# A feed-forward attention tail hosted by the first expert unit, and closer routing stages between two expert units

## What is computed

```python
x = x + 0.5 * ffn(layernorm(x))      # three tree-routed MLPs give q, k, v (16 leaves of width 64),
                                     # then softmax(q k^T / sqrt(128)) v with one head of 128
x = x + attention(layernorm(x))      # 16 heads, rotary positions, alibi, causal
x = x + 0.5 * ffn(layernorm(x))
x = x + 0.5 * moe(layernorm(x))      # softmax gate, top 2 of 8 experts, and a shared MLP; each MLP is
                                     # (silu(x w1) * (x w3)) w2, inner width 256
x = x + mamba(layernorm(x))          # selective scan, 16 states
x = x + 0.5 * moe(layernorm(x))
```

## Time and profile before

| | |
|---|---|
| median of 3 runs | 1473.67 us (1473.6 to 1476.0) |
| the profiled execution | 1469.0 us |
| span of the profiled execution | 1467.2 us |
| granted TensorE clock, mean | 0.945 |
| busy PE / DVE / ACT / POOL | 83% / 68% / 41% / 17% |
| second ffn unit's tail in front of the experts | twice, at 358 and at 1081 us |
| first expert unit of a layer | begins at 369.5, 653.9, 1093.0 and 1377.3 us |
| second expert unit of a layer | begins at 413.8, 697.5, 1137.1 and 1420.9 us |

### The profile page before, as it was taken

How to read it: one execution, slowest core, us unless ns; L and a number is a source line. 1 busy time by engine, 2 the same in 40 slices (tenths; PEclk the granted TensorE clock), 3 DMA queues, 4 the chain that set the end, 5 groups by cost and what they waited for, 6 DMA issues and landing times.

```text
span 1467.2 us, 16299 instructions
## 1 busy us (share of the span) xinstructions
PE 1214.4 (83%) x5655; PEld 743.9 (51%) x5704; DVE 1000.6 (68%) x1944; ACT 596.4 (41%) x995; POOL 242.3 (17%) x211
## 2 busy tenths in 40 slices
PE   5997888998997575669999977889989956747798
PEld 3675444676664122236667644446766622312465
DVE  6666665555685996977764775645557769889765
ACT  4542455344224345422234424543432254455222
POOL 3001000000200461631000010000001015536110
PEclk9999899999999797999999999999999978979999
DMA  6203110001010000010100122100010100000110
GB/s 207 58 25 98 51 55 2 1 1 44 15 58 0 1 0 0 1 58 1 65 23 1 49 54 74 32 2 0 1 58 1 58 1 0 0 0 1 58 62 11
DMA packets 27315, 45.06 MB, mean 31 GB/s; under 512 B 3649, under 2 KB 19297, under 8 KB 27041
## 3 DMA queue, kind: packets, MB, share of 16 engines
q1 hardware_dynamic: 27232, 44.02, 9.5%
HBM read 36.34 MB, written 8.19 MB: 30 GB/s over the span
## 4 chain that ended last, share of the span: by engine, by line
PE 62%; DVE 21%; issue 8%; ACT 5%; DMA 2%; POOL 2%; SPq 1%; POOLq 0%; DVEq 0%; another core or an unknown queue 0%; ACTq 0%
PE bank L1385 12%; PE bank L1387 11%; PE bank L1386 11%; PE bank L1546 8%; DVE n_h L1353 4%; PE bank L1394 3%; DVE a_mx L1291 3%; DVE bank L1345 3%; PE bank L1463 2%; PE bank L1609 2%; PE bank L1519 2%; PE bank L1705 1%; PE bank L1580 1%; POOL n_hc L751 1%; PE bank L1647 1%
## 5 line engine op out<-in xcount | busy, mean ns | idle before, releaser
L1141 DVE SCALAR_TENSOR_TENSOR f_hl<-bank,f_hh 128x512 fp32r<-128x512 f32 x192 | 131.5, 689 | 125.0 <-ACT f_hh L817 124.1
L817 ACT ACTIVATE f_hh<-bank 128x512 fp32r<-128x512 f32 x192 | 114.7, 597 | 197.0 <-PE bank L1463 151.2
L751 POOL TENSOR_TENSOR n_hc<-n_h,n_cs 128x512 f32<-128x512 f32 x128 | 160.4, 1270 | 141.2 <-DVE n_h L1353 93.1
L876 ACT ACTIVATE m_sl<-bank 128x512 f32<-128x512 f32 x144 | 85.8, 597 | 220.0 <-PE bank L1387 219.5
L1385 PE MATMUL bank<-xT_h,mw_h 128*128 128x512 f32 x288 | 160.6, 558 | 7.0 <-DVEq L495 4.3
L1705 PE MATMUL bank<-n_hc,ident 128*128 128x512 f32 x256 | 143.5, 679 | 11.6 <-POOL n_hc L751 10.8
L1353 DVE TENSOR_TENSOR_SCAN n_h<-n_da,bank 128x512 f32<-128x512 f32 x128 | 149.6, 1206 | 4.6 <-POOL n_hc L751 4.5
L1546 PE MATMUL bank<-m_h,mw 128*128 128x512 f32 x288 | 145.6, 594 | 0.0
L969 ACT ACTIVATE n_da<-n_dt,amat 128x512 f32<-128x512 f32 x128 | 91.7, 721 | 131.9 <-DVE n_h L1353 124.9
L1291 DVE TENSOR_REDUCE a_mx<-bank 128x1 f32<-128x384 f32 (+3 forms) x176 | 106.2, 638 | 50.4 <-PE bank L1649 48.0
L1203 DVE TENSOR_TENSOR m_t<-m_sl,bank 128x512 f32<-128x512 f32 x128 | 87.9, 686 | 73.4 <-PE bank L1387 72.8
(11 more groups left out here) (231 smaller groups left out, 2381.2 us busy)
## 6 DMA issues: line engine op xcount, KB each, us to landing
m_c<-comb_dram SPq DMA_DIRECT2D x28, 512.0 KB, 5.0
a_q<-stack_dram SPq DMA_DIRECT2D x8, 512.0 KB, 3.8
a_k<-stack_dram SPq DMA_DIRECT2D x16, 256.0 KB, 5.2
stage_fw<-in_fw_dram SPq DMA_DIRECT2D x6, 512.0 KB, 8.1
stack_dram<-R SPq DMA_DIRECT2D x16, 192.0 KB, 2.9
w_stage<-in_mw_dram SPq DMA_DIRECT2D x9, 256.0 KB, 2.7
stack_dram<-R SPq DMA_DIRECT2D x16, 128.0 KB, 2.6
m_c0b<-comb_dram SPq DMA_DIRECT2D x4, 512.0 KB, 3.4
```

Of the source, the lines that this page charges most:

```text
L751: n_hcs.by(nc.gpsimd.tensor_tensor(n_hc[:, m, :], n_h[:, m, :], n_cs[:, n // 2 % 2, :], ALU.mult))
L817: f_hi.by(act.activation(f_h[0][:, i % 4, :], bank[:, i % 3, :], ACT.Relu))
L1141: f_lo.by(V.scalar_tensor_tensor(f_h[1][:, i % 4, :], bank[:, i % 3, :], 0.0, f_h[0][:, i % 4, :].bitcast(F32), ALU.max, ALU.subtract))
```

## The change

It does two things. First, a second ffn unit that an expert unit follows ends without a barrier, and the expert unit hosts its tail in steps 0 to 7 by the plan above (units 5 to 6 and 17 to 18). The expert unit therefore hosts the stages of its own successor with a lag of 7. Second, where an expert unit hosts the stages of an expert unit (units 6, 10, 18 and 22 host for 7, 11, 19 and 23), the stages stand closer by new tables: ranks and combine are one stage (`choice`), the four exps are one stage of POOL. PSUM banks are dealt anew: product b uses 2 and 7, the w2 sums bank 3 (slot 0) or 6 (slot 1), the turned sums bank 4, the stages bank 5 where the host is an expert unit. Two DMA waits are replaced.

```diff
-POOL_STAGES = {0: "guess", 3: "rms", 8: "exp 0", 9: "exp 1", 10: "exp 2", 11: "exp 3"}
+POOL_STAGES = {0: "guess", 3: "rms"}
+PAIR_DVE_STAGES = {0: "stats", 1: "rows", 4: "low", 6: "first", 8: "fourth", 9: "choice", 10: "row"}
+PAIR_POOL_STAGES = {0: "guess", 6: "exps"}
+PAIR_ACT_STAGES = {4: "high"}
+PAIR_PE_STAGES = {3: "turn", 5: "first", 11: "weights"}
...
-            return UNITS[u] in (("ffn", 0), ("moe", 0), ("mha", 0))
+            return UNITS[u] in (("ffn", 0), ("moe", 0), ("mha", 0)) or tail_follows(u)
+
+        def tail_follows(u):
+
+            return UNITS[u] == ("ffn", 1) and u + 1 < NU and UNITS[u + 1][0] == "moe"
+
+        def moe_lag(u):
+            if UNITS[u][1] == 1:
+                return MOE_LAG
+            return FFN_LAG if tail_follows(u - 1) else 0
+
+        def stage_bank(u):
+
+            return 5 if u and UNITS[u - 1][0] == "moe" else 7
+
+        def y_bank(p):
+            return (3, 6)[p]
+
+        Y_ROWS = 4
...
-                        sp.wait_ge(unit_done, done_before(UNITS_OF_EXPERTS[k]))
+                        sp.wait_ge(m_s2.sem, m_s2.at(k, 8))
+                    if p == 1 and n == 3:
+
+                        sp.wait_ge(m_hs.sem, m_hs.at(k - 1, 14))
...
-                if stage in EXPS and kind == "moe" and UNITS[u - 1][0] == "moe":
-
-                    t = EXPS.index(stage)
+                if stage == "exps":
+
                     pool.wait_ge(e_sub.sem, e_sub.at(k, 0))
-                    e_exp.by(nc.gpsimd.tensor_tensor(gexp[:, t], euler[:, t], glog[:, t], ALU.pow))
+                    for t in range(NT):
+                        e_exp.by(nc.gpsimd.tensor_tensor(gexp[:, t], euler[:, t], glog[:, t], ALU.pow))
...
-                if p == 0:
+                if runs_on(u):
                     return
                 copy_pT(k, 1)
...
-                    hand_over(u, i - MOE_LAG * p)
+                    hand_over(u, i - moe_lag(u))
+                    if tail_follows(u - 1):
+                        kf = kth[u - 1]
+                        if i in (2, 4):
+                            copy_pT(kf, i // 2)
+                            probs(kf, i // 2 + 1)
+                        if i == 6:
+                            copy_pT(kf, 3)
                 act.wait_ge(m_s2.sem, m_s2.at(k, MSTEPS - 1))
-                m_y.by(act.activation(m_yT[:], bank[:, 6, :], ACT.Copy))
+                m_y.by(act.activation(m_yT[:], bank[:, y_bank(p), :], ACT.Copy))
...
+                    if tail_follows(u - 1):
+                        kf = kth[u - 1]
+                        if i == 0:
+                            rows_of_v(kf)
+                        if i in (1, 3):
+                            score_max(kf, 2 + i // 2)
+                        if i == 7:
+                            weighted(kf, batch_of(u - 1))
+                    hand_over(u, i - moe_lag(u))
...
-                if p == 1:
+                if p == 1 and not runs_on(u):
                     attend(k, [item for at in sorted(ATTEND_AT) for item in ATTEND_AT[at]])
...
-                        m_b.by(product(bank[:, 2 + i % 2, :], [mw[c][:, e, 2 + m, :] for c in range(2)], x))
+                        if i == 1:
+
+                            pe.wait_ge(e_row.sem, e_row.at(k, 0))
+                        m_b.by(product(bank[:, (2, 7)[i % 2], :], [mw[c][:, e, 2 + m, :] for c in range(2)], x))
...
-                        if i2 == 0 and p == 1:
-
-                            pe.wait_ge(m_y.sem, m_y.at(k - 1, 0))
-                        m_s2.by(mm(bank[:, 6, :], mw2[:, e, m, :], m_h[:, i2 % 3, :],
+                        if i2 == 0 and tail_follows(u - 1):
+
+                            pe.wait_ge(f_vok.sem, f_vok.at(kth[u - 1], 0))
+                        m_s2.by(mm(bank[:, y_bank(p), :], mw2[:, e, m, :], m_h[:, i2 % 3, :],
                                    start=i2 == 0, stop=i2 == MSTEPS - 1))
-                    if i == 1:
-
-                        pe.wait_ge(e_row.sem, e_row.at(k, 0))
-                    hand_over(u, i - MOE_LAG * p)
+                    if tail_follows(u - 1):
+                        attend(kth[u - 1], ATTEND_AT.get(i, ()))
+                    hand_over(u, i - moe_lag(u))
```

More of the change, by code:

```diff
@@ L121 @@
              5: [("weigh", 0), ("weigh", 1), ("weigh", 2), ("turn", 3)], 7: [("weigh", 3)]}
-EXPS = [f"exp {t}" for t in range(NT)]
 HEAD_PARTS = [f"{side} {c}" for side in "qk" for c in range(3)]
@@ L126, with stage_at @@
 HEAD_LAG = {0: -6, 1: 11}
-def stage_at(table, i, kind):
+def stage_at(table, i, kind, host):
     late = ("turn", "high", "low")
@@ L135, in stage_at @@
                 return ahead.get(i)
+    if kind == "moe" and host == "moe":
+        for own, pair in ((DVE_STAGES, PAIR_DVE_STAGES), (POOL_STAGES, PAIR_POOL_STAGES),
+                          (ACT_STAGES, PAIR_ACT_STAGES), (PE_STAGES, PAIR_PE_STAGES)):
+            if table is own:
+                return pair.get(i)
     if kind == "mamba":
@@ L789, in prologue @@
                     act.wait_ge(g_tr.sem, g_tr.at(u, 0))
-                    g_xh.by(act.activation(xT[0][:, p, :], bank[:, 7, :], ACT.Copy,
+                    g_xh.by(act.activation(xT[0][:, p, :], bank[:, stage_bank(u), :], ACT.Copy,
                                            scale=norm_w if kind == "mamba" else 1.0))
@@ L1099, in prologue @@
                         scores()
-                    if stage == "ranks":
+                    if stage in ("ranks", "choice"):
                         ranks(cmp[p])
-                    if stage == "combine":
+                    if stage in ("combine", "choice"):
                         combine()
@@ L1202, in moe @@
                     if e < EXPERTS:
-                        m_ts.by(V.tensor_tensor(m_t[:, m, :], m_sl[:, m, :], bank[:, 2 + m, :], ALU.mult))
+                        m_ts.by(V.tensor_tensor(m_t[:, m, :], m_sl[:, m, :], bank[:, (2, 7)[m], :], ALU.mult))
                         dve.wait_ge(m_ts.sem, m_ts.at(k, 2 * e + m))
@@ L1412, in prologue @@
                         pe.wait_ge(g_xl.sem, g_xl.at(u, 0))
-                        t_sc.by(product(bank[0:96, 7, :], [rw[0][:, 0:96], rw[1][:, 0:96]], xs(p)))
+                        t_sc.by(product(bank[0:96, stage_bank(u), :], [rw[0][:, 0:96], rw[1][:, 0:96]], xs(p)))
                     if stage == "second":
                         pe.wait_ge(t_bit.sem, t_bit.at(k, 0))
-                        t_cnt.by(mm(bank[:, 7, :], tree[:, 0, :], dbit[:], start=True, stop=True))
+                        t_cnt.by(mm(bank[:, stage_bank(u), :], tree[:, 0, :], dbit[:], start=True, stop=True))
                     if stage in ("third", "fourth"):
@@ L1558, in rows_of_y @@
                 pe.wait_ge(m_y.sem, m_y.at(k, 0))
-                m_ytr.by(back(7, m_yT))
+                m_ytr.by(back(Y_ROWS, m_yT))
             def mha(u, k, p):
```

35 lines of the change are left out of this document (18 added, 17 removed).

## The result

The changed kernel took 1478.09 us (median of 20 runs, 1474.69 to 1481.35), the kernel before on the same chip 1473.84 (20 runs, 1468.96 to 1476.85). The ratio is 1.0034, 95% interval 1.0025 to 1.0043: slower, by 4.3 us between the medians. The forecast was 1472.8 and "no difference".

A forecast was written before the change was run, and what follows sets the result against it. It took a chain of waits to bound the tail and PE the expert steps. 12.0 gained less 6.4, 2.3 and 2.4 lost left 0.9 us gained: 1472.8 us against the 1473.7 median, range 1465.5 to 1479.5.

The forecast's parts named there:

- no difference: Likeliest case for the whole kernel: 0.9 us gained, 1472.8 us, own range 1470 to 1476, chance 0.40.
- The walk of waits: Step-by-step timing of PE, DVE, ACT and POOL through hosted tail and closer stages, giving the 12.0, 6.4 and 2.3 us terms.
- Part 1: Tail of units 5 and 17 hosted in the expert steps behind: 6.0 us gained per place, 12.0 in all.
- Routing wait of DVE: Units 6, 10, 18, 22: DVE waits 2.6 us for POOL's four exps, with its multiplies queued behind.
- PE's waits at the end of unit 6: Units 6 and 18: PE waits 1.1, 1.4 and 0.9 us; 3.2 us lost each, 6.4 in all.
- Low clock behind them: Slow PE clock after the waits ending units 6 and 18: 1.2 us lost each, 2.4 in all.
- Units 10 and 22: Closer stages at lag 0, `first` in step 6: net 1.1 us lost each, 2.3 in all.
- the sum: All terms over the whole kernel: 12.0 - 6.4 - 2.3 - 2.4 = 0.9 us gained.
- The waits are covered: Faster rival, units 6 and 18: clock holds, 3.3 us gained; with exps' wait half as costly, 7.6 us, 1466; chance 0.33.
- ACT's table switches: Slower rival, tile 2's probabilities in step 2: each switch costing twice 1.28 us loses 4.8 us, 1478.5; chance 0.15.
- the slack: Hosted tail, tile 2's Exp before PE's transposes of step 3: 0.45 us to spare, the smallest on the way.
- The routing chain costs more than walked: Slower rival: late DVE also delays the next unit's start, 2 us more in units 6 and 18, 1477; chance 0.12.

The follow-up runs named there:

- e9: Changed kernel plus eight idle matmuls at the head of mamba units 8 and 20: 1475.28 us, ratio 1.0004 to the kernel before.
- e4: Changed kernel with old stages in units 10 and 22, and turn to exps one step earlier in units 6 and 18: 1467.62 us, ratio 0.9943 to before.
- e12: The kernel of e4 plus eleven idle matmuls in PE's waits at the ends of units 6 and 18: 1469.83 us, ratio 0.9963 to the kernel before.

## Why the prediction was wrong

**The walk of waits was right.** Step by step against the profile after:

- First expert matmul right behind unit 5, step 8 23.2 us behind the v copy: as forecast. No wait of PE over 0.3 us in the hosted tail. By the last product of unit 6 the tail's place has gained 6.2 to 6.4 us (6.0). Part 1 stands.
- Routing wait of DVE: 2.48 us (2.6). PE's waits at the end of unit 6: 2.8 us (3.4). Low clock behind them: 1.3 us, from unit 7's 43.54 less 42.20 (1.2).
- Units 6 and 7 together: 1.4 us gained (98.54 less 97.13), 1.3 in 18 and 19. The forecast was 1.6 (6.0 - 3.2 - 1.2).
- Units 10 and 22: 1.2 to 1.5 us lost (1.1; the sum wrote 2.3 for twice that). DVE's wait in unit 10 is 2.48 us too, and PE waits 0.21 and 0.48.

The last of these, two lines of the timeline of PE in unit 10:

```profile
684.40 0.50 PE L1432 MATMUL bank<-xT_h,mw_h 128*128 128x512 f32 x1 [0.21 <-DVE m_t L1242]
687.39 0.60 PE L1441 MATMUL bank<-ident,gbuf 128*8 128x128 f32 x4 [0.48 <-DVE gbuf L1168]
```

Together: 2.7 gained, about 2.7 lost, nothing left, where the sum had 0.9 gained. The means at equal clock say -1.5 with an uncertainty of some us. Both agree with "no difference" as far as the waits go.

**The step that failed is a term that the sum put at nothing without a reason: low clock in the units that the change doesn't touch.** The sum priced low clock at the ends of units 6 and 18 (2.4 us) and behind the tail of before, and nowhere else. At its own places it was right: units 6 and 7 together have 3.4 us at the low level in every profile of either kernel, 18 and 19 too. It only moved, from behind the lone tail to the start of units 7 and 19. Yet the changed kernel has 22 us more at the low clock than the kernel before (208 against 185 in the mean of all runs). So all of the 22 lie elsewhere: a few in units 10 and 22 (8 to 12 us at the low level in each, 3 to 10 before), the rest in code that the change leaves alone. At 0.213 they are worth 4.7 us. The profiles say the same without that figure: outside the units 6, 7, 10, 18, 19 and 22 the changed kernel took 1170.1 to 1176.1 us, the kernel before 1166.0 and 1168.0. With the waits at nothing this makes +4.7, measured +3.3 with an interval of 2.4 to 4.2; the 1.4 between them is within what the arithmetic is good for. The 0.213 comes from executions of one unchanged kernel. That the place of the code alone can move the clock, and the time with it, e9 shows. Why the changed kernel meets more low clock than the kernel before, no run shows, nor could I have forecast the direction from the trace of before.

**The second failing is in the reference.** I carried the 4.7 us from the profiled execution to the median as a constant. They were no constant, but came with 24 us less of low clock in that one execution (5.1 us at 0.213), and they were the sign that a term of some us was at work in a kernel whose expected change was 0.9. The range (1465.5 to 1479.5) held the time by luck: it reached so far up because of the rivals on ACT's table loads and on the routing chain, and neither happened. The likeliest case's own range, 1470 to 1476, did not hold it.

**The rivals.** "The waits are covered" is refuted: the clock did not hold, and DVE's wait is full length. "ACT's table switches" is refuted as a mechanism: a load took 1.28 us and step 8 began on time, though the slack was used up and PE's weight load waited 0.28 us. The Trainium skill, page "ScalarE: Activation LUTs", section "What ACT_TABLE_LOAD costs", would add a drain of about 1380 ns to each load; the trace disagrees, since after the load at 368.70 (1.28 us) the Exp starts at 369.99, and the next load 0.02 us behind its read of the accumulator. "The routing chain costs more than walked" gave 1477, near the time, but by a mechanism that did not happen: PE's waits were shorter than walked.

The Trainium skill, page "TensorE: Matmul & The Clock Gate", section "What's actually happening", says that the number of matmuls at the low clock at a kernel's start differs from run to run, and puts the penalty of that ramp under 1% of a typical span. This case agrees that low clock differs from run to run: a mean clock of 0.930 to 0.947 among 96 executions. But here it is not only at the start, and its price is no smaller than what tuning changes: an estimate from 185 us at 0.213 is 39 us, 2.7% of the span, and the fastest and the slowest of the 96 are 15 us apart, over four times the effect in question.

**The gain that went missing.** Hosting the tail is worth its 6 us per place (6.2 to 6.4 measured at the last product of unit 6). The closer stages and the low clock behind them give most of it back (units 6 and 7 keep 1.2 to 1.4), because two steps of 2.25 us are too short for 6.53 us of exps when the wait stands in front of DVE's multiplies, in the last steps of a unit at that. One step more (e4) takes DVE's wait away and PE's first two, and the kernel beats both, by 8.2 us against the kernel before, part of it by less low clock elsewhere.

## What to carry to other kernels

When a walk of the waits nets out to a thousandth of the time, look at the granted clock of every run, not only at the profile, before a sign is put to the forecast: the same code was up to 15 us apart here. When stages are moved closer to each other, hold the longest operation between them against the distance in steps, and see what is queued behind the engine that waits for it; here one step more gave 4.3 us by the stretches of its units. Where PE must wait at the end of a unit, idle matmuls in the wait can keep the clock up for the next unit (42.18 us instead of 43.54), but they only pay while there is a wait to fill (e12 lost 1.1 us per place with them).

## What the runs showed that I had not expected

- More work made the kernel faster: 8 idle matmuls ahead of units 8 and 20 took 3.0 us off the changed kernel's mean; 16 put 4.5 on, and in the kernel before 8 put 0.9 on.
- In the 96 runs of one kernel, a us at the low clock goes with 0.21 us of time, where in PE-bound unit 7 it costs half of itself (1.3 us for the 2.8 us at the low level).
- Table loads between Silu and Exp cost 1.28 us each and, where one stands between two other activations, nothing on either side (0.02 us). Of the eight added ones PE felt two, by a weight load that waited 0.28 us.
- Three sets of runs of the changed kernel gave 1.0034, 1.0005 and 1.0033. A set's interval did not cover the next set.
